# An attention layer over graph edges, taken by pairs of entries with the heads on the partitions, and the roles of weights and streamed rows exchanged in its sums

## What is computed

```python
def _gat_conv(x, src, dst, W, att_src, att_dst, b, num_nodes, heads):
    h = (x @ W).reshape(num_nodes, heads, C)
    a_src = jnp.sum(h * att_src, axis=-1)
    a_dst = jnp.sum(h * att_dst, axis=-1)
    e = a_src[src] + a_dst[dst]
    e = jnp.where(e > 0, e, NEG_SLOPE * e)
    m = jax.ops.segment_max(e, dst, num_segments=num_nodes)
    ex = jnp.exp(e - m[dst])
    den = jax.ops.segment_sum(ex, dst, num_segments=num_nodes)
    alpha = ex / den[dst]
    msg = h[src] * alpha[:, :, None]
    out = jnp.zeros((num_nodes, heads, C), h.dtype).at[dst].add(msg)
    return jnp.mean(out, axis=1) + b
```

## Time and profile before

| | us |
|---|---|
| median of 3 runs (7335.72 to 7362.3) | 7348.3 |
| span of the profiled execution (first to last instruction) | 7200.7 |
| median less the span, taken as what lies around it | 147.6 |
| PE busy in the span | 5306.6 |
| DVE busy | 4043.0 |
| POOL busy | 3792.6 |
| ACT busy | 2988.5 |
| attention gathers, first to last start | 4492.8 to 7045.6 |

### The profile page before, as it was taken

One profiled execution on the slowest core, in us unless ns is written; L12 is line 12 of the kernel. 1 busy time (PEld: TensorE's weight loads), 2 busy tenths in 40 slices (PEclk: granted clock), 3 DMA queues, 4 the chain that ended last, 5 costly groups with the idle time before them and its releaser, 6 DMA issues. The chain is left out here.

```text
span 7200.7 us, 135903 instructions
## 1 busy us (share of the span) xinstructions
PE 5306.6 (74%) x31642; PEld 4026.1 (56%) x31642; DVE 4043.0 (56%) x12632; ACT 2988.5 (42%) x8170; POOL 3792.6 (53%) x3867
## 2 busy tenths in 40 slices
PE   4777777777777777785888786677777777777774
PEld 3555555555555555543666664566666666566664
DVE  5656656665666666665555555455455555455557
ACT  2444444444444444423666664233333333333335
POOL 3555555555555555502555551666666666666662
PEclk7888888888888888896888886555555555555555
DMA  5433333433334333332111111222222222222222
GB/s 158 106 99 101 100 99 99 102 103 99 101 102 105 100 99 103 100 95 57 39 39 38 38 39 26 44 44 43 44 43 44 44 44 44 44 43 44 43 44 46
DMA packets 531406, 504.25 MB, mean 70 GB/s; under 512 B 328647, under 2 KB 390672, under 8 KB 531023
## 3 DMA queue, kind: packets, MB, share of 16 engines
q0 software_dynamic: 122832, 255.14, 15.7%
q1 hardware_dynamic: 337654, 130.31, 8.6%
q10 hardware_dynamic: 70794, 117.58, 4.9%
HBM read 476.98 MB, written 25.63 MB: 70 GB/s over the span
## 5 line engine op out<-in xcount | busy, mean ns | idle before, releaser
L604 POOL DMA_INDIRECT G<-Atab,ms x1616 | 1577.2, 976 | 1411.2 <-DVE EE L627 523.5
L1840 POOL DMA_INDIRECT Gt<-TAB,metat x1632 | 1606.2, 984 | 1067.2 <-issue 454.6
L1304 POOL DMA_INDIRECT Gc<-XS,metac x560 | 542.1, 968 | 500.9 <-PE Sc L1495 233.4
L2010 PE MATMUL SR<-P,Gt 128*128 128x64 f32 x3264 | 803.8, 428 | 0.0
L701 ACT COPY BS<-BK 128x512 f32<-128x512 f32 x808 | 436.2, 588 | 872.0 <-remote 855.7
L2010 PEld LDWEIGHTS SR<-P,Gt 128*128 128x128 f32 x3264 | 727.1, 328 | 47.8
L1882 DVE TENSOR_REDUCE lt<-MT 128x1 f32<-128x256 f32 x408 | 170.2, 417 | 978.1 <-DMA WB<-Btab 958.2
L662 DVE TENSOR_TENSOR acc<-acc,TT 128x64 f32 (+1 forms) x808 | 178.4, 233 | 862.8 <-remote 534.9
L1998 PE MATMUL PT<-ident,EX 128*128 128x128 f32 x816 | 269.5, 434 | 520.3 <-ACT EX L1960 481.9
L805 PE MATMUL SX<-BS,oh 128*32 128x256 f32 x3232 | 564.7, 475 | 69.6 <-issue 47.3
L754 PE MATMUL SS<-EE,oh 128*32 128x256 f32 x3232 | 571.5, 465 | 48.4 <-issue 46.8
(11 more groups left out here) (288 smaller groups left out, 10615.3 us busy)
## 6 DMA issues: line engine op xcount, KB each, us to landing
mm<-MM ACTq DMA_DIRECT2D x202, 512.0 KB
ZR<-in_eft SPq DMA_DIRECT2D x202, 256.0 KB
Gt<-TAB,metat POOLq DMA_INDIRECT x1632
tb<-DF SPq DMA_DIRECT2D x202, 128.0 KB
G<-Atab,ms POOLq DMA_INDIRECT x1616
dq<-DQ SPq DMA_DIRECT2D x12, 768.0 KB, 5.9
Gc<-XS,metac POOLq DMA_INDIRECT x560
ad<-ADT SPq DMA_DIRECT2D x408, 0.5 KB
```

The source lines that it names most:

```text
L604: e.indirect_dma_start(G[:, k, s, :], None, Atab, bass.IndirectOffsetOnAxis(ap=ms[:, k, s:s + 1], axis=0)).then_inc(l_g[k], 16)
L1304: e.indirect_dma_start(G[:, k, s, :], None, XS, bass.IndirectOffsetOnAxis(ap=meta[:, k, s:s + 1], axis=0)).then_inc(l_g[k], 16)
L1840: e.indirect_dma_start(G[:, k, s, :], None, TAB, bass.IndirectOffsetOnAxis(ap=meta[:, k, s:s + 1], axis=0)).then_inc(l_g[k], 16)
L2010: m = e.matmul(SR[q][:, 0:2 * W], G[:, k, s, 0:128], P[:, q, s * 2 * W:(s + 1) * 2 * W], start=(s == 0), stop=(s == 3))
```

## The change

`phase_gat` takes a pair of entries per iteration, 204 instead of 408 (`load_pairs` reads their number from a table cell that the start of the program now also writes).

- Tiles: `M` has (entry, node, head) on what becomes 128 partitions, one column block for each of the 4 slots of edges; so `MT`, `TE`, `EX`, `P` are 128 x 512 per pair, where they were 128 x 256 per entry. The fold of two slot halves falls away. `Gt` has 4 slots of a pair in place of 8 of an entry, the same bytes.
- POOL issues 8 gathers per iteration, waiting for t5 of the pair four back.
- PE: t1 and t4 make 4 transposes each. t5 is 8 products with 64 columns of `P` as weights and the 128-wide gathered rows streamed, into partitions 0 to 63 (first entry) and 64 to 127 (second) of `UU`. ACT `sums` copies `UU` to `US`, and a new step t6 transposes it into `FR`, beside the spread factors and the row sums.
- DVE `highest` now holds the two score steps too, `maxima` does the running maxima of both entries one after the other and writes them back itself, `update` puts both entries into `acc`.
- The lists: DVE maxima 2, window 1, outside 1, leak 2, masked 1, update 4, highest 1. ACT turned 3, factors 2, weights 2, sums 3, scores 1. PE t2 2, t5 3, t3 2, t1 1, t4 2, t6 3.
- SP loads 64 score values per entry instead of 128.

```diff
             def gather(j):
-                k = j.slot(8)
-                if j.o % 2 == 0:
-                    wait(e, l_mt[k // 2], 48 * j.uses(8))
-                if not j.first(8):
-                    wait(e, s_t5, j.at(-7))
+                k = j.slot(4)
+                wait(e, l_mt[k], 48 * j.uses(4))
+                if not j.first(4):
+                    wait(e, s_t5, j.at(-3))
                 e.sem_inc(s_pool, 1)
-                for s in range(4):
-                    e.indirect_dma_start(G[:, k, s, :], None, TAB,
-                                         bass.IndirectOffsetOnAxis(ap=meta[:, k, s:s + 1], axis=0)).then_inc(l_g[k], 16)
+                for h in range(2):
+                    for s in range(4):
+                        e.indirect_dma_start(G[:, k, s, h, :], None, TAB,
+                                             bass.IndirectOffsetOnAxis(ap=meta[:, k, h, s:s + 1], axis=0)).then_inc(l_g[k], 16)
...
             def t5(j):
-                k, q = j.slot(8), j.slot(2)
+                k, q = j.slot(4), j.slot(2)
                 wait(e, s_p, j.at(1))
+                wait(e, s_us, j.at())
+                for s in range(4):
+                    for h in range(2):
+                        m = e.matmul(UU[64 * h:64 * h + 64, 0:128], P[:, q, s * 128 + 64 * h:s * 128 + 64 * h + 64], G[:, k, s, h, 0:128],
+                                     start=(s == 0), stop=(s == 3))
+                m.then_inc(s_t5, 1)
+
+            def t6(j):
+                k, q = j.slot(4), j.slot(2)
+                wait(e, s_us, j.at(1))
                 if not j.first(2):
-                    wait(e, s_u, j.at(-1))
-                e.matmul(SR[q][:, 2 * W:4 * W], ones[0:1, :], sc[:, j.slot(4), :], start=True, stop=True)
-                e.matmul(SR[q][0:64, 4 * W:6 * W], dsum[:, j.slot(4), :].to_broadcast([128, 64]), i2[:, :],
-                         start=True, stop=True)
-                for s in range(4):
-                    m = e.matmul(SR[q][:, 0:2 * W], G[:, k, s, 0:128], P[:, q, s * 2 * W:(s + 1) * 2 * W],
-                                 start=(s == 0), stop=(s == 3))
-                m.then_inc(s_t5, 1)
-
-            pipeline(e, T, U, D, [(6, t5), (4, t4), (1, t1), (3, t3), (2, t2)])
+                    wait(e, s_u, j.at(-1) * 2)
+                e.transpose(FR[q][:, 0:128], US[:, q, :], ident[:, :])
+                e.matmul(FR[q][:, 128:256], ones[0:1, :], sc[:, k, :], start=True, stop=True)
+                e.matmul(FR[q][0:64, 256:384], dsum[:, k, :].to_broadcast([128, 64]), ident[:, :],
+                         start=True, stop=True).then_inc(s_t6, 1)
+
+            pipeline(e, T, U, D, [(2, t2), (3, t5), (2, t3), (1, t1), (2, t4), (3, t6)])
```

More of the change, by code:

```diff
@@ L1847, in _ @@
             e.memset(neg[:, :], -1.0).then_inc(s_i, 1)
[L1848 to L1851, removed]
+            T = load_pairs(e, tb)
+            regs = [[e.alloc_register(f"g_base{k}{h}") for k in range(4)] for h in range(2)]
             L = lambda b: acc[0:1, 3:5, ds(b, W)]
-            UD = lambda b: ((slice(0, 128), acc[:, 1:3, ds(b, W)], 0), (slice(32, 33), acc[32:33, 3:5, ds(b, W)], 4 * W))
@@ L1932, in _, with update @@
-            pipeline(e, T, U, D, [(1, window), (3, leak), (1, outside), (2, highest), (1, masked), (2, score),
-                                  (7, rescale), (2, leak_score), (7, add), (3, new_max), (3, step_max)])
+            def update(j):
+                q = j.slot(2)
+                bases = [kept(e, regs[h], j) for h in range(2)]
+                wait(e, s_t6, j.at(1))
+                for h in range(2):
+                    b = bases[h]
+                    part = lambda p, o: FR[q][p, o + 64 * h:o + 64 * h + 64].rearrange("p (n h) -> p h n", h=2)
+                    wait(e, s_u, j.at() * 2 + h)
+                    for p, lo, to in ((slice(0, 128), 1, 0), (slice(32, 33), 3, 256)):
+                        a = acc[p, lo:lo + 2, ds(b, W)]
+                        i = e.tensor_tensor(a, a, part(p, 128), ALU.mult)
+                    i.then_inc(s_u1, 1)
+                    wait(e, s_u1, j.at() * 2 + (h + 1))
+                    for p, lo, to in ((slice(0, 128), 1, 0), (slice(32, 33), 3, 256)):
+                        a = acc[p, lo:lo + 2, ds(b, W)]
+                        i = e.tensor_tensor(a, a, part(p, to), ALU.add)
+                    i.then_inc(s_u, 1)
@@ L1935, in _, with scores @@
+            pipeline(e, T, U, D, [(2, maxima), (1, window), (1, outside), (2, leak), (1, masked), (4, update), (1, highest)])
         @blk.scalar
         def _(e):
-            T = load_T(e, tb, 1)
-            def a1(j):
-                k, q = j.slot(8), j.slot(2)
+            T = load_pairs(e, tb)
+            def scores(j):
+                k, q = j.slot(4), j.slot(2)
                 wait(e, s_mx, j.at(1))
+                wait(e, l_mt[k], 48 * j.uses(4))
                 if not j.first(2):
@@ L1996, in t4 @@
                 wait(e, s_ex, j.at(1))
-                for s in range(2):
+                for s in range(4):
                     m = e.transpose(PT[q][:, s * 128:(s + 1) * 128], EX[:, q, s * 128:(s + 1) * 128], ident[:, :])
```

176 lines of the change are left out of this document (80 added, 96 removed).

## The result

The changed kernel takes 7304.5 us (median of 6 runs, 7292.9 to 7328.4), the kernel before 7352.9 beside it (6 runs, 7335.7 to 7374.3): a ratio of 0.9934, interval 0.9916 to 0.9953, 48 us less. On another chip, timed in turns, it was 0.9912 (0.9883 to 0.9940), 62 us less. I had forecast 7770 and "slower": wrong in direction, with 0.7 per cent gained where 5.7 were to be lost. The time lies just inside the range I gave, 7300 to 8250, at an end that only the cheap turns reach.

The account below looks back on a forecast made before the run. Bound: POOL's gather rows, with PE's signals held until the last gather lands. 204 pairs x (14.6 - 12.53) us gave +422 on a span of 7200.7, making 7623; 147.6 around it gave 7770. Range: 7300 to 8250.

Parts of the forecast that it names:

- the cheap turns: Periods in which the product POOL waits for is done when PE's held signals are told: 12.4 us a pair.
- The bound: No engine is full; POOL's row of gathers and the wait behind it set the period, 12.37 us.
- the hold's end: PE's signals, held back while POOL issues gathers, are told once the row's last gather has landed, 1.63 us after its issue.
- What lies around the span: Time outside the profiled span of 7200.7 us, taken as 147.6 us and added to the sum.
- The parts: Engine work per pair after the change: PE 7.0 us, t5 2.1 of it, DVE about 7, ACT 3.6, POOL's gathers unchanged.
- a drain at each change of mode: At t5's two tiling switches a pair on PE: estimated 0.2 us each, making the sum 40 us longer.
- What the order does: PE's list order puts t5 behind held signals of t1 and t4, so periods alternate, mean 14.6 us a pair, +422 us.
- The dear turn: A period in which POOL waits for the chain through maximum, scores, P and t5 after held signals are told: 16.5 us.
- only cheap turns: Rival: t1 and t4 are heard each time, 12.4 to 12.9 us a pair, 7330 to 7450 us; 15 in 100.
- onset of the hold: Moment in POOL's row from which PE's signals are held: between 2.2 and 6.0 us, taken near 4.1.
- POOL's floor: Rival: signals wait for PE's pauses, so POOL gathers without pause, 10.28 us a pair, 6890 us; 17 in 100.
- The swap does nothing: Rival: t5's records run serially, 4.2 us a pair, 7990 us; counted within the forecast, no chance of its own.

Follow-up runs that it names:

- x_t5x2: The changed kernel with t5's product of weights and Gt computed twice over, same result: 7297.8 us, 0.995 of the kernel before.
- x_half: The changed kernel with four of a pair's eight gathers left out after the first four pairs: 6422.2 us, 0.875 of the kernel before.
- x_pause: The changed kernel with POOL waiting, after four of a pair's eight gathers, until these have landed: 7209.3 us, 0.983 of the kernel before.
- x_gap: The changed kernel with POOL clearing 1150 numbers of its own buffer after four gathers of a pair, without waiting for their landing: 7088.3 us, 0.987 of the kernel before.
- z_gapl: The changed kernel with POOL clearing 1700 numbers after four gathers of a pair, a break of about 1.65 us: 7064.9 us, 0.9800 of the kernel before.
- x_tight: The changed kernel with POOL's gathers waiting for t5 of the pair three back, not four: 7179.5 us, 1.000 of the kernel before.
- x_serial: The changed kernel with t5's 16 records ordered by entry instead of by quarter: 7132.8 us, 0.993 of the kernel before.

## Why the prediction was wrong, point by point

**The bound: right.** POOL's row and the wait behind it set the period, 12.38 to 12.40 as I had read it from before. It hardly moves with PE's work (x_t5x2, 0.11 of 1.55 us), and moves with the gathers (x_half) and with where POOL pauses (x_pause, x_gap, z_gapl). What I had of the hold's end, the landing of the row's last gather, is too narrow: in x_gap signals are told though the next gather has begun.

**What lies around the span: wrong**, 147.6 for 1.8 us. The span and the times were from chips of different speed. The sum began at the span of one and ended at the median of the other, so the difference of the kernels, and with it the direction, doesn't hang on it; the periods of the profile were those of the quicker sort.

**The parts: right but for one.** t5 2.1 forecast and 1.98 measured; PE 7.0 forecast, 6.4 measured; DVE 7 forecast and 5.8 measured, ACT 3.6 and 2.6, both hidden. The gathers are unchanged in number, and 0.15 to 0.24 us a pair shorter, which I hadn't forecast: I had costed the halved DVE instructions at nothing, since they are hidden, and this term, put at nothing, is most of the 48 us. Against the Trainium skill, TensorEngine Tiling (Array Packing), "Tiling Modes", from which I drew a drain at each change of mode, the row of t2 ends at 5808.90 and t5 starts at 5808.84, and t3 starts at 5810.74 where t5 ends at 5810.82: nothing of a drain is seen, nor of the 40 us (the ends of PE's records are modelled, but these overlaps of 0.06 and 0.08 are those of its neighbouring records elsewhere, 0.08 between t2 and the product before it).

**"What the order does": the step that failed.** I walked from a release with t5 still to do, and put t1 4.2 and t4 5.2 us into the next row, held, so that each second turn would be dear, +2.0 us a pair. Three things were wrong in it. First, t4 needs only what is told at the release itself (t3's result), so it runs 0.4 to 1.5 us into the row and passes in every regular turn; I had put it behind t1, which stands before it in the list but has already run when the release comes (5812.68 to 5813.80, release 5817.22). Second, t1 may be held at no cost, because its pair is needed a row later. Third, t5's own signal is held in every turn and still comes in time, since POOL asks for it at the very release that tells it. So the chain that must pass between two releases is t4 to P and t2 to the maxima, and both are done within the first 3.35 us of the row. The dear turn, forecast at +4.1 us in every second pair, is absent: in place of 14.6 us a pair there are 12.40. And there is slack: with one pair less of it (x_tight) the period grew by 0.15 us, not by 6.

**The rival "only cheap turns"** (15 in 100, 7330 to 7450) is what came true, 26 us below its edge (12.4 a pair gives 7322 by my own sum, not 7330). I let it hang on an onset of the hold later than 5.2 us into the row. The rival needs only that 3.35 us pass, and 3.8 do: t2 of x_tight is done at 5814.30 in a row begun at 5810.50, and `ln` starts 0.7 later with DVE's own 1.56 us of idle time before it. Above, 5.8 us (t3) is held in the regular turns. But **no fixed onset fits all rows**. Of each twelve pairs of the changed kernel two have other stops of POOL. After a stop of 3.90 us t2 is done 6.56 us into the row, and DVE's 2.07 us of idle time is no more than without a hold:

```profile
4811.63 0.95 POOL L1846 DMA_INDIRECT Gt<-TAB,metat  x1 [3.90 <-remote]
...
4817.82 0.37 PE L1985 MATMUL RW<-ident,lt 128*1 128x128 f32 x1
...
4819.41 0.21 DVE L1900 TENSOR_TENSOR ln<-acc,RW 1x64 f32<-1x64 f32 x1 [2.07 <-PE RW L1985]
```

And where POOL stops for 1.86 us behind a single gather and then issues 15 in a row (from 5833.03), t3 is done 3.0 us into them, heard 2.96 us later, and heard in the midst of the gathers:

```profile
5835.44 0.58 PE L1989 MATMUL RW<-neg,ln 1*128 1x1 f32 x2
...
5838.98 0.16 ACT L1950 COPY nl<-RW 128x1 f32<-128x1 f32 x1 [3.57 <-remote]
```

So how late a signal is depends on the stops before the row too, and a held signal need not wait for the row's end.

**POOL's floor** came true on no holding chip, and the reason I gave it (signals that wait for PE's pauses) is refuted. "The swap does nothing", priced at 7990, did not come true: t5 became shorter, and where it is slower (x_serial, 2.88 us) the period stays.

## What to carry to other kernels

Where signals are told in bursts, sort the steps by the burst at which their input is told and the burst at which their result is needed; a step that is held costs nothing unless its result is needed before the next burst, and the order in the list says little by itself. A period set so doesn't shrink with the work inside it: with a third less PE work the kernel gained 0.7% here, and most of that came from shorter gathers. When an engine's row of issues delays everyone, try a short break or an early wait inside it, and look at more than one chip before a tuned break is kept: the long break gave 0.980 on a chip that holds signals, and shorter, more frequent breaks cost 1.015 to 1.064 on the one that doesn't.

## What the hardware showed that I had not expected

- The same kernel took 7315 to 7374, 7172 to 7215 or 5604 us by chip; the difference goes with how PE's signals come through while POOL gathers.
- On the holding chips, in the regular turns, a signal of PE up to 3.35 us into a row of gathers is heard within 0.2 us, and one of 5.8 us and later mostly 1.8 to 1.9 us behind the end of the row's last gather. After a longer stop of POOL (3.90 us) one 6.56 us into the row came through. What resource is behind this stays open; breaks of 1.2 us let signals through after four gathers and not after eight.
- Lengthening t5 changed PE's granted clock, with no simple rule. Over 4600 to 7000 it was 0.50 in the changed kernel (above). The stretch 5000 to 6000 with t5 twice, the same with its records in series, the 16 records in series themselves, and PE in the kernel before:

```profile
5000.00:6000.00 1000.00, 603.02 (x3834) 469.27 (x3834) 465.13 (x1752) 208.71 (x560) 611.36 (x638) 0.63 0.20 43
```
```profile
5000.00:6000.00 1000.00, 571.36 (x2571) 424.85 (x2571) 467.37 (x1763) 211.41 (x566) 621.66 (x647) 0.56 0.21 44
```
```profile
5808.50:5811.50 3.00, 3.00 (x18) 2.62 (x17) 2.41 (x10) 0.31 (x1) 2.09 (x3) 0.50 0.22 46
```
```profile
5812.74:5821.12 8.38, 8.38 (x34) 6.92 (x34) 4.01 (x19) 2.40 (x9) 6.04 (x7) 0.50 0.27 49
```

In the changed kernel PE works for 6.5 us of each 12.4, in one piece of 5.4 (5805.94 to 5811.32) and one of 1.1, at its lower level of 1.2 GHz throughout. In the two others t5 makes the long piece 0.9 to 1.6 us longer, and part of the time is granted at the upper level of 2.4 GHz. But longer unbroken work isn't enough: the kernel before has pieces of 8.4 us (last row) and more work in all, and stays at 0.50. What makes the difference is open.
